# Graph network kernel: in the attention stage, VectorE's logit sums and the first layer's activation stand between its first three message multiplications of a group

## The reference, cut to what matters

```python
h = (x @ W).reshape(N, H, C)
e = a_src[src] + a_dst[dst]                      # logit of each edge (and of a self loop)
e = where(e > 0, e, 0.2 * e)
alpha = exp(e - e_max[dst]);  alpha = alpha / segment_sum(alpha, dst)[dst]
agg = segment_sum(h[src] * alpha[:, :, None], dst)
out = elu(agg + bias + x @ skip_W)
```

```python
w = silu(silu(edge_attr @ fc_w1) @ fc_w2) @ fc_w3    # 64, 64, 256 columns, scales left out
```

## Time and profile before

| | us |
|---|---|
| median of 3 runs | 6132.24 |
| the profiled execution, its own time | 6131.38 |
| its span, first to last instruction | 6129.7 |
| attention stage: first message multiplications of the first and of the last group | 178.0 and 2323.4 |

### The profile page before, as it was taken

One profiled execution on the slowest core, in us unless ns is written; L12 is line 12 of the kernel. 1 busy time (PEld: TensorE's weight loads), 2 busy tenths in 40 slices (PEclk: granted clock), 3 DMA queues, 4 the chain that ended last, 5 costly groups with the idle time before them and its releaser, 6 DMA issues.

```text
span 6129.7 us, 211599 instructions
## 1 busy us (share of the span) xinstructions
PE 5670.6 (93%) x41086; PEld 4585.1 (75%) x41087; DVE 5468.8 (89%) x17616; ACT 3388.1 (55%) x12391; POOL 4638.9 (76%) x3959
## 2 busy tenths in 40 slices
PE   6899999999999997779999999999999999999966
PEld 5555555555555555669999999999999999999844
DVE  2899999999999997879999999999999999999888
ACT  2566666666666665555555555555555555555522
POOL 2777777777777773338888888888888888888877
PEclk9899999999999999999999999999999999999999
DMA  6799999999999995459999999999999999999998
GB/s 200 223 266 270 266 269 267 268 269 267 269 268 268 268 267 157 142 137 178 178 178 178 178 176 176 178 176 178 177 179 178 176 177 178 178 178 179 162 305 288
DMA packets 1269403, 1298.04 MB, mean 212 GB/s; under 512 B 220911, under 2 KB 1180656, under 8 KB 1269264
## 3 DMA queue, kind: packets, MB, share of 16 engines
q1 hardware_dynamic: 941186, 829.31, 46.5%
q0 software_dynamic: 328176, 468.28, 44.6%
HBM read 695.20 MB, written 601.74 MB: 212 GB/s over the span
## 4 chain that ended last, share of the span: by engine, by line
PE 66%; issue 10%; DVE 8%; DMA 5%; SPq 5%; POOL 3%; DVEq 2%; ACT 0%; POOLq 0%; ACTq 0%
PE PS L988 12%; PE PS L970 11%; PE PS L883 10%; PE PS L959 8%; PE PS L1003 8%; PE PS L873 6%; PE PS L986 5%; DMA part<-arena,c_idx 4%; SPq L429 2%; DVE big L1241 2%; DVE big L1179 1%; PE PS L824 1%; DVEq L354 1%; DVE big L1187 1%; DVE arena L1268 1%
## 5 line engine op out<-in xcount | busy, mean ns | idle before, releaser
L596 POOL DMA_INDIRECT part<-arena,c_idx x1664 | 2588.6, 1556 | 533.9 <-issue 438.2
L566 POOL DMA_INDIRECT big<-h_tab,big x1664 | 1635.8, 983 | 515.4 <-issue 397.0
L883 PE MATMUL PS<-big 128*128 128x260 f32 x3328 | 972.1, 411 | 151.5 <-DVE big L1179 135.9
L988 PE MATMUL PS<-w2m,arena 128*128 128x128 f32 x6656 | 1104.9, 289 | 0.0
L883 PEld LDWEIGHTS PS<-big 128*128 128x128 f32 x3328 | 556.7, 189 | 437.1 <-issue 324.4
L988 PEld LDWEIGHTS PS<-w2m,arena 128*128 128x128 f32 x6656 | 877.3, 192 | 0.0
L970 PE MATMUL PS<-arena 128*128 128x256 f32 x3328 | 858.2, 381 | 12.8 <-ACT arena L776 12.0
L1187 DVE TENSOR_TENSOR big<-big,PS 128x260 f32 x1664 | 703.0, 422 | 172.7 <-PE PS L883 117.8
L673 ACT ACTIVATE big<-PS,arena 128x128 f32<-128x128 f32 x1664 | 512.0, 358 | 524.2 <-PE PS L873 523.8
L752 ACT COPY arena<-PS 128x384 f32<-128x384 f32 x1664 | 716.8, 483 | 38.3 <-PE PS L959 4.4
L1003 PE MATMUL PS<-big,arena 128*128 x4992 | 683.2, 273 | 5.0 <-DMA arena<-ot_tab 5.0
(11 more groups left out here) (181 smaller groups left out, 10898.2 us busy)
## 6 DMA issues: line engine op xcount, KB each, us to landing
w_tab<-big SPq DMA_DIRECT2D x416, 520.0 KB
arena<-w_tab SPq DMA_DIRECT2D x1664, 130.0 KB
part<-arena SPq DMA_DIRECT2D x1664, 32.1 KB
ot_tab<-big SPq DMA_DIRECT2D x416, 128.0 KB
arena<-ot_tab SPq DMA_DIRECT2D x416, 128.0 KB
arena<-src_tab SPq DMA_DIRECT2D x416, 128.0 KB
arena<-part SPq DMA_DIRECT2D x392, 128.5 KB, 3.4
big<-h_tab,big POOLq DMA_INDIRECT x1664
```

What stands on the lines that cost most here:

```text
L566: pool.indirect_dma_start(hg[:, s, k, :], None, h_tab, bass.IndirectOffsetOnAxis(ap=sidx[:, s, k:k + 1], axis=0)).then_inc(s_hg[s], 16)
L596: pool.indirect_dma_start(part[q], bass.IndirectOffsetOnAxis(ap=c_idx[:, s, k:k + 1], axis=0), o_cmb[:, s, k, :], None, compute_op=ALU.add ...
L883: mm(PS[:, 2 + k % 2, 0:HW], oh[:, p, k, :], hg[:, p, k, :], start=True, stop=True).then_inc(s_agg, 1)
L988: last = mm(o_v[:, k, 2 * j:2 * j + 2, :].rearrange("p j u -> p (j u)"), midT[:, k, 1 + j, :], w2m[:, (1 + 2 * j) * MUL:(3 + 2 * j) * MUL] ...
```

## The change

Two pieces of VectorE's step are moved ahead. The logit sums (4 in the list above) stand between `message(0)` and `message(1)`, and h1 (5) between `message(1)` and `message(2)`. Their waits move with them. The loading of block numbers and the addition of the self loop keep their place behind `message(2)`, and so they now stand behind the logit sums and h1. Nothing else differs.

```diff
@@ -1190,7 +1190,18 @@
                 if there(g - 2):
                     wait(dve, s_p, g - 1)
                     message(0)
+                if there(g - 1):
+                    wait(dve, s_ad, g)
+                    v.tensor_reduce(ad[:, m % 2, :, :],
+                                    PS[:, 1, 0:GROUP * 6 * H].rearrange("p (k i j) -> p k j i", k=GROUP, i=3),
+                                    AX.X, ALU.add).then_inc(s_z, 1)
+                if there(g - 2):
                     message(1)
+                if there(g):
+                    wait(dve, s_t1, g + 1)
+                    wait(dve, s_f2, g - 1)
+                    half_silu(h1[:, s % 2, :], t1[:, s % 2, :], PS[:, 6, 0:2 * P]).then_inc(s_h1, 1)
+                if there(g - 2):
                     message(2)
                     b = numbers(dve, block_row, (g - 2) * GROUP, GROUP, NB)
                 if s == 3 and own is not None:
@@ -1198,15 +1209,6 @@
                     wait(dve, s_acc, GROUP * (g - 2))
                     x = acc[:, ds(own, 1), 0:D].rearrange("p o d -> p (o d)")
                     v.tensor_tensor(x, x, own_h[:, :], ALU.add).then_inc(s_own, 1)
-                if there(g - 1):
-                    wait(dve, s_ad, g)
-                    v.tensor_reduce(ad[:, m % 2, :, :],
-                                    PS[:, 1, 0:GROUP * 6 * H].rearrange("p (k i j) -> p k j i", k=GROUP, i=3),
-                                    AX.X, ALU.add).then_inc(s_z, 1)
-                if there(g):
-                    wait(dve, s_t1, g + 1)
-                    wait(dve, s_f2, g - 1)
-                    half_silu(h1[:, s % 2, :], t1[:, s % 2, :], PS[:, 6, 0:2 * P]).then_inc(s_h1, 1)
                 if there(g - 1):
                     wait(dve, s_hg[m], landed(g - 1, m, GROUP))
                     wait(dve, s_z, 5 * g - 4)
```

## The result

| | before | after |
|---|---|---|
| median us (7 runs each) | 6140.79 (6131.7 to 6145.16) | 6164.32 (6153.47 to 6172.01) |
| the profiled execution, its own time | 6131.38 | 6165.57 |
| attention stage, first message(0) of the first to that of the last group | 2145.5 | 2165.5 |
| everything behind it | 3806.3 | 3820.3 |

The change makes the kernel slower: 1.0038 times the time before, 95% interval 1.0028 to 1.0048, so 17 to 29 us. The forecast was 66 us. The sign was right and the size was not: about a third of it came, and 6164.32 us lies under the forecast's own range of 6180 to 6215.

The account below looks back on a forecast made before the run. TensorE and VectorE were taken as close to full, in a loop of waits of 5.14 us a step. Terms of 3, 11, 12, 28 and 12 made 66 us on 6131.38, so 6198 us for the median, range 6180 to 6215.

Parts of the forecast that it names:

- (h): Self-loop steps: a late ScalarE tanh now holds h1's earlier turn, delaying load and self loop's add; 12 us.
- (f): Self loop's add: block-number loads over 0.475 us delay it past its turn; 12 us.
- (e): Plain steps: block-number loads over 0.68 us delay add_up(0) beyond the idle time before add_up(2); 11 us.
- (a): Logit sums moved earlier: their wait for L907 ends in time, so free.
- (c): message(2) starts 0.5 us later but ends well before sums(2) starts: hidden.
- (b): message(1) 0.17 us later may delay sums(1) on TensorE, on the loop; 0.01 us in 318 steps, 3 us.
- (d): VectorE's stream: h1's wait for ScalarE's tanh holds back the block-number load, which starts 0.72 us after message(0).
- rival E: TensorE's start after the later message(1) decides: 19 to 57 us for it, 6213 to 6251 us in all; chance 0.12.
- rival B: The block-number load isn't held back by h1's wait or exposed, so its costs go: 6163 us; chance 0.20.
- (g): Self-loop steps: add_up(0)'s wait for s_own is no longer covered; 0.29 us in 98 steps, 28 us.
- Rival C: The waits, above all for s_own before add_up(0), are absorbed: +10 us, 6142 us; chance 0.09.

Follow-up runs that it names:

- late_after_3: Changed kernel with SyncE's four zero fills cut to one a step and the self loop's rows loaded one step later; 6288.25 us, ratio 1.0225.
- own_behind_h1: Kernel before with only the self loop's add moved behind h1, right ahead of L1213; 6169.88 us, ratio 1.0035.
- sums_only_3: Kernel before with only the logit sums moved between message(0) and message(1), third execution; 6152.15 us, ratio 1.0007.
- own_ahead: Changed kernel with the self loop's add moved between message(1) and h1; 6151.75 us, ratio 1.0009 against before.
- numbers_first: Changed kernel with only the load of block numbers moved directly behind message(0); 6170.54 us, ratio 1.0047 against before.
- zero_after: Changed kernel with SyncE's four zero fills of a step made one transfer; 6157.41 us, ratio 1.002 against before.
- zero_before: Kernel before with SyncE's four zero fills of a step made one transfer; 6127.62 us, ratio 0.997.
- zero_own_ahead: Changed kernel with the self loop's add between message(1) and h1 and SyncE's zero fills cut to one a step; 6135.68 us, ratio 0.9989 against before.

## Why the prediction was wrong, step by step

The step that failed is the counts that went into (h), (f) and (e), 35 us together: they priced late tanhs and long loads as if the changed kernel had as many as the kernel before. Beside them a term of the other sign was missing. One by one:

**(a), (c)** were free, as said. **(b), 3 us.** The weights of sums(1) are loaded at 0.970 instead of 0.868 after message(0), and its first pass ends at 1.468 in both. It cost nothing; rival E falls.

**(d)** held. The load starts at 0.735. The rule of the Trainium skill (page "Perfetto Trace Analysis", section "Sequencer Loop") would leave it ahead of message(0), and neither this trace nor late_after_3, where it follows the tanh at 1.538, shows that. So of rival B, whose 6163 us (31 over before) came nearest to the result (23 over), one reason did not hold, as the load does stand behind h1's wait. Its other reason did: only the tail of the loads counts, and their lengths belong to the place where the load stood (below). It too left out what the longer loop gives back, the 8 us between 31 and 23.

**(g), 28 us,** was the price. The idle time of 0.23 behind L1215, add_up(0) at 2.237 (2.24 forecast), the step 5.428 (5.43), sums(3) 0.32 late, add_up(3) 0.29: as worked out. own_behind_h1 shows it alone. One number inside was off: sums(2) starts 0.15 us after add_up(0) has ended and not 0.25, and ends 0.10 late, where 0.24 was forecast; the way over sums(3) decided anyway. Rival C falls.

**(h), 12 us, failed,** and so did **(f), 12,** and **(e), 11.** The mechanisms are real: late_after_3 shows (h), sums_only_3 (f), own_ahead (e). What failed is what I fed them. "Read step by step, 25 of the 98 have the tanh later than 0.75" and "a mean of 0.49, with 30% over 0.475" are counts of the trace of before, and I took them over as if they were constants of the kernel. After the change none of the 98 has a late tanh, and 24 of 416 loads are over 0.475. (h) is 0. For (e) and (f) together numbers_first leaves nothing that can be told from zero; the sum of s 3 is 532.8 against 531.6 in zero_after, so about 1 us.

The two counts went for different reasons. The late rows, and the late tanhs with them, go with the longer loop: own_behind_h1, as slow as after, has none either. The long loads do not: own_behind_h1 has its load in the old place and a mean step of 5.210, and 251 of its 416 loads are over 0.475, more than before. numbers_first, with the load back ahead of message(0), has 205. What took them away in after is that the change itself moved the load by 1.29 us.

**The term that was missing** is what a longer loop gives back. The kernel before had two bounds within half a per cent: the loop of TensorE and VectorE at 5.148 a step, and SyncE's issue at 5.17. I named the first and took the second for scattered waits of ScalarE. A change that makes the loop's mean 5.22 (a quarter of 0.29 on top) passes SyncE and pays only from there: s 2 gives back 5.6 us, and the late rows go. The other 3.4 us come back in s 0, where the gathers no longer start with message(0) (last section; a relation read off traces, no run moved the gathers alone). So the stage's +20.0 is 26.9 - 5.6 - 3.4 - 0.1 over 392 steps, and 2.2 in the first and last steps, which I haven't followed up. The sum I should have written is 28 - 9 = 19 us, 6151 us; the measured median ratio gives 23 (17 to 29).

What sets the length of the load into registers stays open. In the traces it is long where it starts 1 to 2.5 us behind SyncE's issue of the w_tab store (in own_behind_h1 1.09 us on average 1.0 to 1.5 us behind it, 0.36 from 3 us on). In before 127 loads start 1 to 2.5 us behind it, with a mean of 0.71 us; in after 3 do, and 385 start 3 us or more behind it, with a mean of 0.38. Both the load's place in the step and SyncE's lag go into that distance, which is why own_ahead, with the place of after and another lag, has 202 loads over 0.475. That is a relation read off traces; no run changed one without the other.

## What to carry to other kernels

Before taking the count of late transfers from a trace, look whether some queue never waits: then it sets the pace together with the loop, a slower loop takes the late transfers away again, and the first hundredths of a step that a change costs are free. Before taking the lengths of an instruction that the change moves, ask whether they belong to the place where it stood. When an instruction that signals is moved, add up everything between it and the one that waits for its signal, and which of those wait in turn: the same add was covered by logit sums, h1 and L1213, cost 0.29 us a step behind L1215 alone, and 0.41 with the logit sums between, because L1214 waits for them. And an open wait stops all that an engine's stream has behind it, register loads too, so a wait moved ahead moves them back.

## What the runs showed of the hardware that was not expected

- VectorE's instructions are longer when a gather of GpSimd starts beside them. In before, s 0, the gather starts with message(0), 3 ns after it in the median, and message(0) takes 0.456 us in the median and 0.418 in other steps; the minimum of s 3, with a gather starting 1 ns after it in the median, takes 0.206 and not 0.168. The timeline of before in such a place, GpSimd then VectorE:

```profile
1513.66 0.95 POOL L566 DMA_INDIRECT big<-h_tab,big  x1 [0.30 <-issue]
1513.66 1.12 DVE L1179 TENSOR_TENSOR big<-big 128x256 f32<-128x256 f32 x3
```

  Three messages take 1.12 here and 1.09 in the earlier trace rows. It is on the loop: s 0 takes 5.180, also in zero_before. In after the gathers fall elsewhere (0.17, 1.54, 2.80 and 4.06 after message(0) in s 1 and s 2, the first at 0.13 in s 0) and s 0 takes 5.142. The Trainium skill, page "SBUF — State Buffer", section "Who interferes with whom", has VectorE and GpSimd, under conditions that it names, take a shared pair of ports in turn, the later one standing for the other's whole instruction. The lines above don't show so much: beside a gather of 0.95 us a message is 0.04 us longer.
- The minimum alone is held by the last part of a gather. Over all the traces, 565 minima start 0.18 to 0.40 us before a gather ends, and 563 of them end with it, within 0.02 us, instead of after 0.168; messages in such a place keep their 0.42.
- The same neighbourhood can lock: in zero_own_ahead oh is 0.05 us longer in nearly every step, and the stage is 2155.8 where zero_before has 2141.1.
- A load of four numbers into registers takes 0.34 to 1.26 us, with medians of 0.34 to 0.72 by kernel.
- SyncE needs 0.35 to 0.38 us for the issue of one transfer and about 0.2 until the next; the four clearing transfers alone take 2.66 of a step's 5.14. That makes a queue of nine small transfers a bound of its own.
